# Graph attention turn: both halves of Y made together, weights computed ahead of the copies

## The reference

```python
x = _layernorm(x + layer0(x))
# layer 1, for all edges and one loop per node
h = (x @ W).reshape(N, 4, 64)
logits = leaky_relu(a_src[src] + a_dst[dst], 0.2)
ex = exp(logits - segment_max(logits, dst)[dst])
alpha = ex / (segment_sum(ex, dst)[dst] + 1e-16)
out = segment_sum(h[src] * alpha[:, :, None], dst).mean(axis=1) + bias
x = _layernorm(x + out)
```

## Time and profile before

| | |
|---|---|
| profiled execution, time | 9740.62 us |
| its span, first to last instruction | 9738.8 us |
| median of 3 runs | 9740.73 us |
| busy: POOL / PE / DVE / ACT | 74% / 64% / 61% / 41% |
| granted TensorE clock, mean | 0.834 |
| layer 0's turns | about 240 to 4500 us |
| layer 1's super steps | about 4800 to 9400 us |

### The profile page before, as it was taken

The page is one execution under the profiler, slowest core; times in us unless marked ns, Lnnn a source line. Parts: engine busy times, 40 slices in busy tenths (PEclk is TensorE's granted clock), DMA queues, the critical chain, the costliest instruction groups (busy, mean ns, idle before and its releaser), DMA issues.

```text
span 9738.8 us, 216685 instructions
## 1 busy us (share of the span) xinstructions
PE 6272.6 (64%) x47166; PEld 4775.6 (49%) x47167; DVE 5903.3 (61%) x14312; ACT 3977.2 (41%) x11056; POOL 7217.9 (74%) x9417
## 2 busy tenths in 40 slices
PE   3466676676676677665366666666666666666675
PEld 2355555555555555553244444444444544445454
DVE  4355555555555555555377777777777777777753
ACT  1344444444444444443144444443443444444431
POOL 0788888888888888881588888888888888888810
PEclk6788888888888888886688888888888888888875
DMA  3111111111111111110311111111111111111100
GB/s 67 38 38 38 38 38 38 38 38 38 38 38 38 38 38 38 38 38 7 33 27 26 27 26 26 27 26 27 26 27 27 26 27 26 27 27 26 27 6 13
DMA packets 301605, 303.34 MB, mean 31 GB/s; under 512 B 194201, under 2 KB 197606, under 8 KB 301064
## 3 DMA queue, kind: packets, MB, share of 16 engines
q0 software_dynamic: 200704, 265.33, 15.4%
q1 hardware_dynamic: 98580, 32.69, 1.9%
q10 hardware_dynamic: 2068, 3.20, 0.1%
HBM read 286.10 MB, written 16.30 MB: 31 GB/s over the span
## 4 chain that ended last, share of the span: by engine, by line
POOL 56%; issue 21%; PE 9%; DVE 4%; POOLq 3%; ACT 2%; DMA 2%; DVEq 2%; ACTq 0%; SPq 0%
POOL big L364 53%; POOL breath L374 3%; POOLq L355 2%; PE ps L795 2%; DVE S L472 1%; DMA big<-q_dram,idx 1%; PE pu L809 1%; PE ps L832 1%; PE ps L827 1%; ACT rowX L996 1%; ACT ST L984 1%; PE pu L944 1%; PE ps L819 1%; PE pu L946 1%; PE ps L783 1%
## 5 line engine op out<-in xcount | busy, mean ns | idle before, releaser
L364 POOL DMA_INDIRECT big<-x_dram,idx x3136 | 3636.4, 1160 | 1064.1 <-issue 848.5
L364 POOL DMA_INDIRECT big<-q_dram,idx x3136 | 3223.4, 1028 | 1022.3 <-issue 791.3
L899 PE MATMUL pu<-Y,S 128*128 128x265 f32 x7856 | 2218.4, 429 | 475.8 <-DVE Y L643 445.5
L984 ACT COPY ST<-ps 128x512 bf16<-128x512 bf16 x1956 | 1071.9, 586 | 2255.8 <-PE ps L795 2179.2
L899 PEld LDWEIGHTS pu<-Y,S 128*128 128x128 f32 x7856 | 1537.4, 206 | 777.8 <-issue 513.9
L795 PE MATMUL ps<-identb,S 128*128 128x128 bf16 x7824 | 1106.2, 233 | 777.3 <-DVE S L472 769.0
L643 DVE TENSOR_TENSOR Y<-big,wb 128x1040 f32<-128x1040 f32 x982 | 1214.4, 1237 | 492.6 <-ACT wb L1070 406.4
L795 PEld LDWEIGHTS ps<-identb,S 128*128 x7824 | 753.0, 96 | 1281.4 <-issue 1058.8
L809 PE MATMUL pu<-rowX,S 128*128 128x192 bf16 x3936 | 585.2, 264 | 1219.9 <-issue 975.0
L472 DVE TENSOR_TENSOR S<-iota,rel 128x1024 bf16 x978 | 1206.6, 1234 | 224.9 <-DVE rel L469 224.3
L509 DVE TENSOR_TENSOR Y<-Y,rowX 128x512 f32<-128x512 f32 x491 | 340.0, 693 | 1459.4 <-ACT rowX L996 1455.8
(11 more groups left out here) (164 smaller groups left out, 8319.1 us busy)
## 6 DMA issues: line engine op xcount, KB each, us to landing
big<-q_dram,idx POOLq DMA_INDIRECT x3136
big<-x_dram,idx POOLq DMA_INDIRECT x3136
rowD<-dst_dram SPq DMA_DIRECT2D x196, 32.0 KB
q_dram<-state SPq DMA_DIRECT2D x3, 1568.0 KB, 20.3
x_dram<-big SPq DMA_DIRECT2D x1, 3381.0 KB, 40.9
idx<-srcT_dram SPq DMA_DIRECT2D x98, 32.0 KB, 1.8
dstc<-dstT_dram SPq DMA_DIRECT2D x98, 32.0 KB
out<-big SPq DMA_DIRECT2D x1, 3104.0 KB
```

Source lines behind the costliest of these rows:

```text
L364: nc.gpsimd.indirect_dma_start(o, None, x_dram if l else q_dram, bass.IndirectOffsetOnAxis(ap=idx[:, half, t:t + 1], axis=0)).then_inc(gat ...
L899: last = t_.matmul(bank, Sf[:, t, :], Y[:, t, :], start=(t == 0), stop=(t == 7))
L984: a_.copy(ST[:, h * 4:h * 4 + 4, :], ps[h][:, 0:2 * P].bitcast(bf16).rearrange("p (t n) -> p t n", t=4)).then_inc(L[k.l][f"sts{h}"], 1)
```

## The change

In layer 1's turn three orders change. VectorE makes half 1 of Y directly behind half 0, at the head of its turn, instead of behind S. ScalarE computes `wb` at the head of its turn, after dw of the same turn, instead of at its end; `ends` of half 1 moves from the head of the next turn to the end of this one, behind the ST copies, so semaphore sf1 has lag 1 instead of 2. TensorE runs the sums of half 1 directly behind those of half 0, ahead of the transposes.

```diff
@@ VectorE turn1
                         weigh(k, 0, at)
+                        weigh(k, 1, at)
...
                         onehot(k, half, (k.sn % 2) * TG)
-                    if k.has(2):
-                        weigh(k, 1, at)
@@ TensorE turn
                     sums(k, 0)
+                    sums(k, 1)
                 if k.has(0):
                     transposes(k, (k.sn % 2) * TG)
-                if k.has(2):
-                    sums(k, 1)
@@ ScalarE
-            act_tiles = Past(act, "act_tile", 2, 2 * TS - TG)
+            act_tiles = Past(act, "act_tile", 1, 2 * TS - TG)
@@ ScalarE turn1
-                    if k.has(2):
-                        ends(k, 1, 2)
+                    if k.has(1):
+                        k.after("dw", 1)
+                        k.after("y1", 2)
+                        a_.activation(wb[:, :, :], dw[:, :, :], ACT.Exp).then_inc(m["w"], 1)
...
                     if k.has(1):
-                        ends(k, 0, 1)
+                        ends(k, 0)
                     if k.has(0):
                         to_sbuf(k)
                     if k.has(1):
-                        k.after("y1", 2)
-                        a_.activation(wb[:, :, :], dw[:, :, :], ACT.Exp).then_inc(m["w"], 1)
+                        ends(k, 1)
```

More of the change, by code:

```diff
@@ L1032, in _, with ends @@
             copied(tab1, D)
-            act_tiles = Past(act, "act_tile", 2, 2 * TS - TG)
+            act_tiles = Past(act, "act_tile", 1, 2 * TS - TG)
             act_blocks = Past(act, "act_block", 3, NB - 1)
-            def ends(k, h, back):
-                k.after(f"U{h}", back + 1)
-                at = act_tiles.back(back - max(k.tail, 0))
+            def ends(k, h):
+                k.after(f"U{h}", 2)
+                at = act_tiles.back(1 - max(k.tail, 0))
                 a_.copy(Y[:, h * 4:h * 4 + 4, UW:YW], edgeE[:, ds(at + h * 4, 4), :])
-                a_.copy(Sf[:, h * 4:h * 4 + 4, :], S[:, ds(((k.sn + back) % 2) * TG + 4 * h, 4), :]
+                a_.copy(Sf[:, h * 4:h * 4 + 4, :], S[:, ds(((k.sn + 1) % 2) * TG + 4 * h, 4), :]
                         ).then_inc(L[1][f"sf{h}"], 1)
@@ L1057, in turn @@
                         a_.copy(Mx[:, ds(b, 1), :], mnew[:, :].unsqueeze(1)).then_inc(m["mb"], 1)
-                    if k.has(3):
                         k.after("e", 3)
```

## The result

The changed kernel takes **9893.76 us** (median of 3 runs, 9892.29 to 9914.31) against 9740.73: a ratio of 1.0165 [1.0141, 1.0188], 153 us slower. The forecast was 9908, so sign and size came out. The mechanism did not: in the mean over layer 1 a gather costs what it did before, and another engine became the bound.

A forecast was written before the change was run, and what follows sets the result against it. The prediction took POOL's gathers, some held by VectorE operations, as layer 1's bound. From 9740.6 us, +171 for longer holds ((1.5 - 1.15) x 489) and -4 for the last super step's shorter turns gave 9908 us, range 9710 to 10,070.

The forecast's parts named there:

- 14 + 10 x 7.3 = 87 us against 94 leaves POOL the bound: Layer 1 super step: answer to the rival that the bound leaves POOL, which got no chance of its own.
- that cover is gone: TensorE's moved sums no longer overlap the ST copies and register work; 2.15 us from copies to next sums.
- 0.35 us a turn for held gathers, +171 us: POOL in layer 1: held time rises from 1.15 to 1.5 us a turn, over 489 turns.
- VectorE's turn 7.0 or 6.3, the wait for wb gone: Layer 1 turn by VectorE: 7.0 us where a new group begins, 6.3 otherwise; the 0.91 us wait goes.
- TensorE's loop 7.3: Layer 1: sums 2 x 1.68, transposes to copies' end 1.77, copy wait and register work 2.15; 0.3 above VectorE's 7.0.
- Gathers held to the end of a VectorE operation: POOL: a gather starting inside a long VectorE operation lasts until about 0.8 us past its end; undisturbed ones take 0.94.
- Five gathers a turn before, 1.02 us held: Old 7.27 us turn: five undisturbed gathers need 6.25 us, and POOL loses the remaining 1.02 at the second Y product.
- Mean gather 1.25, VectorE's wait for gathers up to 13 us a super step: Signs expected in the changed profile: mean gather near 1.25 us, VectorE's wait up from 6.7 to about 13 us.
- Four gathers in a turn: First rival: TensorE's lag never delays VectorE, every turn fits four gathers, 1.95 us held; +391 us, 10,128 us; chance 0.16.
- faster past S: Rival: gathers slip past VectorE's S, five fit in a 7.1 us turn, 0.85 held; -147 us, 9590 us; chance 0.12.
- no change: Rival: turn settles at 7.3 us through TensorE's loop with five gathers; -50 to +20, about 9720 us; chance 0.14.
- the forecast's mix: Half the turns 7.0 us with four gathers, half 7.3 with five; 1.5 us held a turn; chance 0.58.

The follow-up runs named there:

- e2: Kernel before the change with half of layer 1's gathers left out: 10,914.73 us, ratio 0.87.
- e1: Changed kernel with half of layer 1's gathers left out: 11,366.17 us, ratio 0.906.
- g2: Kernel before the change with half of layer 1's gathers left out and TensorE's gaps filled with unread products: 9385.49 us, ratio 0.9637.
- g1: Changed kernel with half of layer 1's gathers left out and TensorE's gaps filled with unread products: 9359.79 us, ratio 0.961.
- e3: Changed kernel with all gathers and TensorE's gaps filled with unread products: 12,629.24 us, ratio 1.0069.
- f2: Changed kernel with all gathers and TensorE's gaps filled with unread products, run again on another chip: 12,648.99 us, ratio 1.0054.

## Why the prediction was right, and where it was wrong

**The step that failed** is the one that closed the rivals: "14 + 10 x 7.3 = 87 us against 94 leaves POOL the bound". The 7.3 holds for a turn at full clock alone. The slow clock was seen, but not put into the loop: a window with a mean clock of 0.79 was read as a disturbance that lets VectorE wait 0.3 us. At 1.2 GHz the sums' 3.4 us become 6.4, and the loop 10.3. POOL ceases to be the bound when the mean turn passes (94.3 - 13.8) / 10 = 8.05 us, that is when a share (8.05 - 7.3) / (10.26 - 7.3) = 0.25 of the turns has slow sums. In the kernel before 98 of 440 turns, 0.22, had a mean clock under 0.85; with that share, each at the full new price, the estimate is 13.8 + 10 x (0.78 x 7.3 + 0.22 x 10.26) = 93.3 us a super step, just under POOL's 94.3. So the trace of before would have told that the bound was within reach, but not that the share would rise: measured are 238 of 440, a mean turn of 8.41 and 97.6 us. The rival that I waved off in one line was the outcome, and for want of a price for the slow turn it got no chance.

**The second step** is "that cover is gone" for the moved sums. I priced it as register work laid bare, 2.15 us, which was right. What it also took away was TensorE's work in the middle of the turn: before, TensorE paused twice in a turn, 1.32 us ahead of the transposes and 0.75 ahead of the first sums, and had some of its light work between the two halves of the sums; now all sixteen sums follow a light stretch and a pause of 1.93. The usual slow turn of before lasts 8.4 us, with some 7 of its 16 loads slow; that of after lasts 10.2, and two stretches above show all 16 slow: the block of sums stays at the lower clock to its end. The experiments show that the pauses are where the slow turns come from: filled, turns of 10.2 us vanish, and with half of the gathers the loss does too.

**The number was right by luck.** I charged POOL with 0.35 us a turn for held gathers, +171 us. In the mean over layer 1 POOL paid nothing: its gather is 1.168 us, its other idle time, without the wait for Y, (839.7 - 115.7) / 2929 = 0.247, a memset 0.059, together 1.474, and 64 of them 94.3 us a super step, as before. The super step grew by 3.5 us since the turns, now 8.4 us on average, fill it: 14 + 10 x 8.4 = 98. (The 14 itself is 15.1 on average now, from 13.8.) Of that POOL's own wait for y1 is 115.7 us over 46 super steps, 2.5 us each; the rest stays unassigned. Both ways came to some +3.5 us a super step, for no common reason.

**Point by point.**
- *VectorE's turn 7.0 or 6.3, the wait for wb gone:* the wait is gone, and turns of 6.9 exist (71 of 440). ScalarE now waits for dw instead (1319.8 us over 461 turns), which costs nothing.
- *TensorE's loop 7.3:* right at full clock, term by term. In the changed trace the copies end at 7013.38 + 1.07 = 7014.45, the first register work of L252 starts at 7014.51, and the next sums start at 7016.60, 2.15 after the copies, the 2.15 of the sum. The rule of the Trainium skill ("Perfetto Trace Analysis", DVE / Act Engine Instruction), by which the sequencer goes on past a waiting instruction, is again not what the trace shows for this register work.
- *Gathers held to the end of a VectorE operation:* seen again. The gather at 7014.14 starts 0.84 us into the Y product of 7013.30 and ends at 15.35, 0.81 behind that product's end. In the fast turns it costs what was forecast and more: the gathers of the 116 turns of 7.2 or 7.3 us take 1.28 us on average, where those of before take 1.19. But the gathers of the 123 turns of 10.2 or 10.3 us take 1.07 (VectorE idles 2.03 and 1.62 us ahead of the two products there), and the mean over all stays at 1.16.
- *Five gathers a turn before, 1.02 us held:* roughly so, 4.8 gathers a turn in the 324 turns of 7.2 or 7.3 us. The turn of the earlier trace rows itself has a second held gather, 1.87 us from 7008.41 in the first Y product, which the working left out.
- *Mean gather 1.25, VectorE's wait for gathers up to 13 us a super step:* both wrong over the whole, 1.163 and nearly none. *Super steps 97.8 apart:* 97.6, by the other way.
- *"Wrong if the mean gather is below 1.16, ... or if POOL shows waits of its own":* the latter holds, and by that test the prediction's account is wrong.
- *Four gathers in a turn, faster past S, no change:* all three rivals take POOL for the bound, and none occurred as a whole. The fast turns of the changed kernel do have about four gathers each (4.2 in those of 7.2 or 7.3 us, 3.7 in those of 6.4 to 7.0), as the forecast's mix and the first rival had it; the turns of 10.2 us, with 7.2, make up for them.

**What is shown and what argued.** Shown: the clock falls with the new order, with and without POOL's load (0.83 to 0.70 in e2 and e1, 0.86 to 0.78 with all gathers); TensorE's loop took POOL's place as the bound of layer 1; with the pauses filled, the turns of 10.2 us are gone, and with half of the gathers the loss too. Not shown: what the changed kernel with all gathers would take at full clock, where the held gathers of the fast turns count again. Argued only: that the pause's place ahead of the sums, not its length alone, makes the light stretch get the full clock and the heavy one the lower. The Trainium skill ("TensorE: Matmul & The Clock Gate", A second HAM failure mode: psum-queue depth-cycling) tells of a kernel whose short idle times between groups of matmuls let the clock swing between both levels; this trace agrees, 0.78 on average with pauses of 1.93 and 0.64 us in each turn. Open: why the changed kernel's turns are longer in e1 than with all gathers (9.14 us against 8.41). Fewer gathers and another session changed together there; e2's turns are longer too (8.13 against 7.48), g2's, in the quicker session, are not (7.42).

## What to carry to other kernels

An engine that is not the bound is so only at the clock that it gets: before you dismiss it, work out its loop at 1.2 GHz too, and what share of slow turns would make it the bound. An edit that gathers scattered TensorE work into one block also gathers its pauses; look at what the engine does right ahead of its heaviest stretch. A forecast that hits the number is tested by its intermediate quantities (here the mean gather and who waits for whom), not by the number. And a mean can hide two opposite halves: here held gathers in fast turns and free ones in slow turns.

## What the runs showed of the hardware

- In successive turns of 10.26 us with a pause of 1.93 us ahead of the sums, the granted clock was in step with the loop: 0.52 to 0.54 over the sums, 0.90 over the light stretch between them, so that the mean over both understates what it costs. The same products took 6.35 us of loads at the one level and 3.44 at the other.
- Products that nobody reads raised the granted clock: with half of the gathers it is 0.70 between 5500 and 8500 us in e1 and 0.93 in g1, and the mean turn 9.14 and 7.19 us, though TensorE has nine more products a turn. The two runs are of different sessions; turns of 10.2 us vanish with the filler in both (e3, f2 and g1).
